# Delta-rule recurrence on one core: beta-k reads the state, the inverse is applied in compact form, and each step's data comes in one record

## The reference, cut to what matters

```python
T = jnp.tril(Bi @ KiT, k=-1)
inv = jnp.linalg.inv(eyeC + T)
Ui = inv @ (Vi - Bi @ W_t)
W_new = W_t + KiT @ Ui
...
O_i = Qi @ W_avg * a + Qi @ W_t * c + T_mat * (Qi @ KiT) @ Ui
```

## Time and profile before

| what | us |
|---|---|
| median of three runs | 1509.95 |
| lowest and highest of them | 1496.23, 1513.25 |
| the profiled execution, its own time | 1498.91 |
| its span, first to last instruction | 1497.1 |

### The profile page before, as it was taken

How to read it: one execution, slowest core, us unless ns; L and a number is a source line. 1 busy time by engine, 2 the same in 40 slices (tenths; PEclk the granted TensorE clock), 3 DMA queues, 4 the chain that set the end, 5 groups by cost and what they waited for, 6 DMA issues and landing times. The chain is left out here.

```text
span 1497.1 us, 35306 instructions
## 1 busy us (share of the span) xinstructions
PE 1164.3 (78%) x14558; PEld 796.8 (53%) x14558; DVE 749.3 (50%) x1707; ACT 452.9 (30%) x889; POOL 321.9 (22%) x309
## 2 busy tenths in 40 slices
PE   4843765665655067778887878999999999999997
PEld 2632434434444056666676764665566666666664
DVE  4689999899999436754444453112111121211111
ACT  3540534424435022222332323331122222222221
POOL 3686101000000011110011104661022222222222
PEclk9875777778778557687888878999999999999999
DMA  7642555464556676567665619952132222223222
GB/s 272 189 145 63 147 153 116 132 162 103 143 111 158 160 158 152 130 143 165 157 148 141 160 56 342 346 167 78 28 47 47 46 47 44 46 47 47 47 46 29
DMA packets 232444, 184.00 MB, mean 123 GB/s; under 512 B 148165, under 2 KB 196197, under 8 KB 227937
## 3 DMA queue, kind: packets, MB, share of 16 engines
q1 hardware_dynamic: 198000, 149.20, 38.0%
q0 software_dynamic: 16368, 19.96, 7.6%
q10 hardware_dynamic: 17920, 12.59, 3.1%
HBM read 101.69 MB, written 86.26 MB: 126 GB/s over the span
## 5 line engine op out<-in xcount | busy, mean ns | idle before, releaser
L1420 DVE TENSOR_TENSOR hid_all<-p_s,silu 128x512 f32<-128x512 f32 x103 | 71.3, 692 | 378.5 <-PE p_s L1271 249.7
L1470 POOL DMA_INDIRECT out_h<-y_sb,x_in x71 | 110.8, 1560 | 360.7 <-DVE y_sb L1432 342.8
L1328 ACT ACTIVATE silu<-p_m 128x512 f32<-128x512 f32 x103 | 61.5, 597 | 328.2 <-PE p_m L1264 223.4
L175 DVE TENSOR_TENSOR xt<-xt,prod 128x62 f32<-128x62 f32 (+15 forms) x248 | 151.8, 612 | 4.3
L1286 PE MATMUL p_y<-wo,hid_all 128*128 x568 | 134.4, 380 | 0.8 <-ACT hid_all L1345 0.8
L1264 PE MATMUL p_m<-wi,xT_c 128*128 x284 | 133.6, 593 | 0.5 <-ACT xT_c L1341 0.5
L1271 PE MATMUL p_s<-ws,xT_c 128*128 x284 | 133.6, 593 | 0.0
L172 DVE TENSOR_TENSOR prod<-nx,xt 128x62 f32<-128x62 f32 (+15 forms) x248 | 129.6, 523 | 2.6
L577 DVE SCALAR_TENSOR_TENSOR cv<-raw,conv_sb,cv 128x512 f32<-128x512 f32 x144 | 107.0, 747 | 18.0 <-ACT raw L493 17.2
L1286 PEld LDWEIGHTS p_y<-wo,hid_all 128*128 128x128 f32 x568 | 102.5, 190 | 12.3 <-issue 1.4
L452 PE MATMUL p_g<-kqM,kT 32*32 32x128 f32 x2048 | 50.7, 369 | 71.2 <-DVE sT L647 53.8
(11 more groups left out here) (139 smaller groups left out, 1938.0 us busy)
## 6 DMA issues: line engine op xcount, KB each, us to landing
slots_in_dram<-h SPq DMA_DIRECT2D x9, 1040.0 KB, 10.0
x_in<-slots_in_dram SPq DMA_DIRECT2D x71, 130.0 KB, 2.1
k_tokens_dram<-kk SPq DMA_DIRECT2D x32, 256.0 KB
chunk_gram_dram<-ng SPq DMA_DIRECT2D x32, 256.0 KB
beta_kv_dram<-bv SPq DMA_DIRECT2D x32, 256.0 KB
nx<-chunk_gram_dram SPq DMA_DIRECT2D x8, 1024.0 KB, 4.9
xt<-in_const SPq DMA_DIRECT2D x8, 1024.0 KB, 8.0
scores_dram<-sT SPq DMA_DIRECT2D x32, 256.0 KB
```

Source lines behind the costliest of these rows:

```text
L175: ins = dve.tensor_tensor(kept, kept, pr, ALU.add)
L1420: dve.tensor_tensor(dst, p_s[n % 2][:], silu[n % 2][:], ALU.mult).then_inc(S["hid_ready"], 1)
L1470: pool.indirect_dma_start(token_rows, bass.IndirectOffsetOnAxis(x_in[s % X_IN][:, D:D + 1].bitcast(U32), 0), y_sb[s % 2][:], None, compute ...
```

## The change

- The projections make beta k and beta v in tensors of their own (`bk`, `bv`). After `gram(b, 1)` TensorE transposes beta k (`turn_beta_k`, 8 transposes into `p_p`), ScalarE copies it out with a minus sign into `nkT` (two copies of 128x512), and SP stores it by channels (`kT_dram`, four stores of 128 KB) after the scores. `project(b + 1, 0)` and `project(b + 1, 1)` wait for these copies in place of those of `kk`.
- k with its copy, scores, inverse and beta v of a chunk lie beside each other in one DRAM tensor: a record of 1792 f32 (7168 B) for each token.
- A step's record comes in one transfer into one of three buffers (`load_record`), after `inside` of three steps earlier. Every fourth step `load_kq` issues 4 loads of minus beta k by channels and 8 of q. POOL now zeroes `nk`, and only the first `load_kq` waits for it.
- `read_k(s)` multiplies minus beta k by the state into `p_r`; VectorE adds beta v (`rho_out`); `apply(s)` multiplies the compact transposed inverse by the result, one 32x32 product for each head and lane, into `p_u`. In chunk 0 there is no `read_k`, and `apply` takes beta v itself.
- `yz`, `take_z`, `read_y`, `yz_out`, `xbd`, and the constants that pick z and sign y go. `turn_xn` uses `p_r`.
- The orders change: `read_k`, `read_q` before `route`; `turn_xn` ahead of `project`; `norm` a step later; `head_norm` ahead of `residual`; `store_inverse` of the last sequence at s = 12 in place of 14.

The diff, cut to its core:

```diff
+AT_KK, AT_SCORES, AT_INVERSE, AT_BV, RECORD = 0, 2 * D, 2 * D + H * C, 2 * D + 2 * H * C, 3 * D + 2 * H * C
...
+    step_dram = nc.dram_tensor("step_records_dram", [NC_BATCH, B, C, RECORD], F32, kind="Internal").ap()
...
                         sp.wait_ge(s_sT, b * TILES + TILES)
-                        by_chunk(sT_dram, b, sT[:].rearrange("p t g x -> p t (g x)"), s_st)
+                        by_chunk(AT_SCORES, b, sT[:].rearrange("p t g x -> p t (g x)"), H * C)
+                        sp.wait_ge(s_nk, b * 2 + 2)
+                        by_slot(kT_dram, b, nkT)
...
                         elif b:
-                            pe.wait_ge(s_kt, (b - 1) * 2 + n + 1)
-                            pe.wait_ge(s_ktri, (b - 1) * TILES + 2 * (n + 1))
+                            pe.wait_ge(s_nk, (b - 1) * 2 + n + 1)
...
+                    def turn_beta_k(b):
+                        for u in range(2):
+                            pe.wait_ge(s_kt, b * 2 + u + 1)
+                            pe.wait_ge(s_ktri, b * TILES + 2 * (u + 1))
+                            pe.wait_ge(s_bk, b * 2 + u + 1)
+                            for s in range(4):
+                                t, k = 2 * u + s // 2, s % 2
+                                ins = pe.transpose(p_p[u][:, s * P:(s + 1) * P], bk[:, t, k * P:(k + 1) * P], ident)
+                            ins.then_inc(s_bkt, 1)
...
                         gram(b, 1)
+                        turn_beta_k(b)
...
+                        for u in range(2):
+                            act.wait_ge(s_bkt, b * 2 + u + 1)
+                            act.activation(nkT[:, :, 2 * u * P:(2 * u + 2) * P].rearrange("p k (t l) -> p t k l", t=2),
+                                           p_p[u][:].rearrange("p (t k l) -> p t k l", t=2, k=KH), ACT.Copy, scale=-1.0
+                                           ).then_inc(s_nk, 1)
...
+                        for f in range(4):
+                            sp.dma_start(nk[i][C * f:C * f + DH], kT_dram[n // TILES, n % TILES, f * DH:(f + 1) * DH]).then_inc(s_nk[i], 16)
...
+                    def load_record(s):
+                        if s >= RING:
+                            sp.wait_ge(S["o_summed"], s - RING + 1)
+                        b = s // NC_BATCH * GROUP
+                        sp.dma_start(record[s % RING][:], step_dram[chunk(s), b:b + GROUP].rearrange("b i x -> (b i) x")
+                                     ).then_inc(s_rec[s % RING], 16)
...
-                        load_yz(s)
-                        load_kk(s)
-                        load_scores(s)
+                        load_record(s)
                         if s == 0:
-                            load_q(0)
+                            sp.wait_ge(s_zeroed, 2)
+                            load_kq(0)
...
+                    def read_k(s):
+                        if chunk(s) == 0:
+                            return
+                        n4 = s // TILES
+                        pe.wait_ge(s_nk[n4 % 2], 16 * 4 * (n4 // 2 + 1))
+                        pe.wait_ge(S["state_ready"], 2 * states(s - 1))
+                        if s >= 3:
+                            pe.wait_ge(S["xnT_ready"], s - 2)
+                        tok = slice(s % TILES * C, s % TILES * C + C)
                         for n in range(HQ):
-                            for f in range(4):
-                                ins = pe.matmul(p_yz[C * f:C * f + C, n, :], bv[s % 2][:, 4 * n + f, :], xbd[s % 2][:, 4 * n + f, :],
-                                                start=True, stop=True)
-                        ins.then_inc(S["yz_summed"], 1)
+                            for b in range(GROUP):
+                                ins = pe.matmul(p_rf[lane(b), n * 4 * DH:(n + 1) * 4 * DH], nk[n4 % 2][:, b, n, tok],
+                                                state[s % 2][:, b, n, :], start=(n == 0), stop=True, skip_group_check=True)
+                        ins.then_inc(S["r_summed"], 1)
...
+                    def apply(s):
+                        pe.wait_ge(s_rec[s % RING], 16 * (s // RING + 1))
+                        if chunk(s):
+                            pe.wait_ge(S["rho_ready"], reads(s))
                         if s:
                             pe.wait_ge(S["u_ready"], s)
-                        for n in range(HQ):
+                        src = rho[s % 2] if chunk(s) else bv[s % RING]
+                        for hd in range(H):
                             for b in range(GROUP):
-                                ins = pe.matmul(p_u[lane(b), n * 4 * DH:(n + 1) * 4 * DH], yz_ch[s % 2][:, n, lane(b)], table("pick_z"),
-                                                start=(n == 0), stop=False, skip_group_check=True)
...
+                                ins = pe.matmul(p_u[lane(b), hd * DH:(hd + 1) * DH], xT[s % RING][lane(b), hd, :],
+                                                src[lane(b), hd * DH:(hd + 1) * DH], start=(hd == 0), stop=True, skip_group_check=True)
                         ins.then_inc(S["u_summed"], 1)
...
-                    yz(0)
-                    take_z(0)
                     for s in range(NT + 4):
+                        if s < NT:
+                            read_k(s)
+                            read_q(s)
                         if s >= 4:
                             route(s - 4)
                         if s < NT:
-                            read_y(s)
-                            read_q(s)
+                            apply(s)
                         if 1 <= s <= NT:
                             turn_o(s - 1)
                         if s < NT:
                             grow(s)
-                            if s + 1 < NT:
-                                yz(s + 1)
                             inside(s)
+                        if 2 <= s < NT + 2:
+                            turn_xn(s - 2)
                         if 1 <= s <= NT:
                             project(s - 1)
-                        if s + 1 < NT:
-                            take_z(s + 1)
-                        if 2 <= s < NT + 2:
-                            turn_xn(s - 2)
...
+                    def rho_out(s):
+                        if chunk(s) == 0:
+                            return
+                        dve.wait_ge(S["r_summed"], reads(s))
+                        dve.wait_ge(s_rec[s % RING], 16 * (s // RING + 1))
+                        if s >= 2:
+                            dve.wait_ge(S["u_summed"], s - 1)
+                        dve.tensor_tensor(rho[s % 2][:], p_rf, bv[s % RING], ALU.add).then_inc(S["rho_ready"], 1)
...
                     for s in range(NT + 4):
+                        if s < NT:
+                            rho_out(s)
+                        solve(SHARE * s)
+                        if 2 <= s < NT + 2:
+                            norm(s - 2)
                         if s >= 4:
                             gate(s - 4)
-                        solve(SHARE * s)
+                        solve(SHARE * s + 2)
                         if s < NT:
                             state_out(s)
+                            solve(SHARE * s + 4)
                             head_sum(s)
-                        solve(SHARE * s + 2)
+                            solve(SHARE * s + 6)
+                            head_norm(s)
                         if 1 <= s <= NT:
                             residual(s - 1)
-                        solve(SHARE * s + 4)
-                        if s < NT:
-                            head_norm(s)
-                        solve(SHARE * s + 6)
-                        if 1 <= s <= NT:
-                            norm(s - 1)
```

196 lines of the change are left out of this document (75 added, 121 removed).

## The result

The changed kernel takes 1566.86 us (median of four runs, 1565.13 to 1570.09) against 1506.69 for the kernel before, measured beside it (four runs, 1496.23 to 1513.25): a ratio of 1.041, with an interval of 1.034 to 1.047. The prediction was 1522, with a range to 1560.

A forecast was written before the change was run, and what follows sets the result against it. TensorE waiting for blocks of 256 instructions was taken to bound the recurrence. +22 us there and net 0 at its start (projections' +4 included) on 1498.9 gave about 1520, 1531 on the median's footing; stated 1522, range 1484 to 1560.

The forecast's parts named there:

- the median's footing: Whole kernel: the sum counted from the three-run median 1509.95 us, not the profiled execution's 1498.9, giving 1531.
- point 1: Recurrence: TensorE groups removed 95.6 us, added 75.0, so busy time falls by 20.6 us, 0.66 us a step.
- point 2: Recurrence: 128 more TensorE instructions a step, 22,912 in place of 18,816, so 91 block refills for 74 or 75.
- point 3: Recurrence: the refill sets the pace almost always; 89 blocks at 4.05 us are 360 us, +22; bounds -13 and +71.
- The clock: Recurrence: more time at the lower clock lengthens work, not refills, which still set the pace; no change counted.
- point 5: Recurrence loads: one record transfer and three buffers gain 0 directly, add no wait; VectorE's new order costs nothing.
- fourth rival: Recurrence: 7 KB record rows hold refills up, 4.6 us a block, +71, 1570 us; chance 0.08.
- points 4 and 5: Recurrence: `read_q`'s 5.0 us wait for o_n goes, not counted as gain; VectorE's new order costed at nothing.
- points 6 and 7: Projections: beta k's transposes and added stores cost together +4 us; recurrence start: net 0, bounds -5 and +3.
- within 1%: Whole kernel: time within 1% of the median shown, from the even case and the forecast's low end; chance 0.33.
- the forecast: Recurrence: 3.98 to 4.3 us a block, 1514 to 1545 around 1522 us; chance 0.37.
- the even case: Recurrence: at 3.85 to 3.95 us a block work and instructions cancel, +4 to +13, about 1506; chance 0.28.

The follow-up runs named there:

- later runs: The kernels before and after, both unedited, profiled again beside the follow-up experiments: 1541.45 us (0.999) and 1598.86 us (1.036).
- b_plus128: Kernel before with 32 more groups of 32x32 products (128 instructions) behind `inside` in each step, results unread: 1602.34 us, ratio 1.040.
- a_minus128: Kernel after with `inside` for 8 of its 16 heads except in chunk 0, 128 instructions a step less: 1566.39 us, ratio 1.014.
- b_same: Kernel before, unedited, measured and profiled again beside the follow-up experiments: 1541.45 us, ratio 0.999.
- a_diag: Kernel after with `apply` as 16 products 128x128 by 128x16 with the block-diagonal inverse, in place of 64 small ones: 1649.38 us, ratio 1.069.
- b_narrow: Kernel before with `project` on 64 of its 256 columns, as many instructions: 1545.95 us, ratio 1.000.
- b_merged: Kernel before with VectorE's new order, without `take_z`; VectorE puts the pick of z into a second, negated state: 1552.58 us, ratio 1.005.
- a_apart: Kernel after with `read_q` behind `apply`, and `turn_xn` and `project` between `grow` and `inside`, same instructions: 1652.60 us, ratio 1.070.
- a_four: Kernel after with each record loaded in four transfers (pieces of 2, 2, 2 and 1 KB), same bytes: 1582.99 us, ratio 1.024.
- a_quiet: Kernel after without the record loads of steps 3 to 31, which reuse the records of steps 0 to 2: 1579.96 us, ratio 1.023.
- b_record: Kernel before, own algorithm, with one record of 8 KB rows in one transfer a step, three buffers, POOL spreading the inverse: 1552.56 us, ratio 1.005.
- b_order_fill: Kernel before with VectorE's new order and one unread product 128x128 by 128x256 more in each step: 1540.22 us, ratio 0.998.

## Why the prediction was wrong

The direction was as written; the size was short by 45 us (1567 for 1522), beyond the range to 1560. 1522 was itself a step between two footings: the sum on the median's footing was 1531, and on that footing 36 us are missing.

- *TensorE's work* (point 1): removed and added groups came out 20 us apart in the later runs, as worked out. That the busy sum of the stage would fall by 20 us was wrong: +47 in the first profiles, +25 in the later ones.
- *Instructions* (point 2): 89 packets for the 91 forecast, gaps in `apply` and `inside`, 90.7 us of issue for "80 or more". Right. (The "about 745" instructions a step do not follow from the count beside it: 22,912 over 32 steps are 716; the trace has 721.)
- *The price of a block* (point 3): the sum said +22 us. b_plus128 gives 16.7 us of waiting for 15 blocks, a_minus128 gives 9.6. The size was near, but not by the mechanism: "the refill sets the pace almost always" was wrong. Only 47 of the 89 blocks were waited for, and between them stand stretches such as the one of 5.85 us in which TensorE never stops. TensorE is busy 320.5 of the 407.3 us, so longer work lengthens the stage too; a step took 13.6 us, not 11.5 to 12. The page "Runtime: NRT & Kernel Launch" of the Trainium skill, in its section on instruction fetch mechanics, has the fetch hidden by the issue rate; the traces of this case disagree: b_same has 44.3 us of issue waits in 28 places, and even a_diag, which has the fewest, 16.4 us in 14.
- *The clock* is the step that failed: "A larger share at the lower level lengthens work, not refills, and the refill still sets the pace; I count no change". In its place the runs show that the lower clock (0.60 for 0.79 in the first profiles, 0.62 for 0.74 in the later ones) lengthened the groups that stay by 44 us in the later runs, and that the refills did not cover it: busy time rose by 24.8 us net, and the rest did not fall but rose by 34.9. The earlier trace rows gave 0.77 and the earlier trace rows windows from 1.00 down to 0.78, so both levels were in the trace of before, and `grow` at both of its durations too: the price of a full fall could have been bounded from it. What in the change makes the clock fall stays open. b_narrow and b_merged show a fall when work is narrowed or taken out in the kernel before, and this change does take work out; a_apart shows one with more waits and another order, and the change brings more waits as well. No run parts the two in the kernel after.
- *One transfer* (point 5): "Gain 0 directly" was wrong by a cost of 16 us. That cost rests on a_four and a_quiet; in b_record, with the algorithm of before, 8 KB rows cost next to nothing. The fourth rival, big packets, had +71 and 1570 us, and the profiles show +72.0 and the median 1567. That is luck: by the runs the transfer accounts for about 16 us of it, and the clock, which that rival does not have, for more. The second half, three buffers, was right: 0.
- *VectorE's order* (points 4 and 5): put at nothing, gave 6 to 9 us in the kernel before. The waits for o_n, said to go, are 3.4 us in three places in the profile of after, for 5.0.
- *Projections and start* (points 6 and 7): +4 and 0 were forecast. The channel loads' buffer is zeroed 6.3 us earlier than the old one (509.63 for 515.89 in the earlier trace rows), and the second u comes 2.2 us earlier (541.36 for 543.62), 6.9 in the later runs. But the first u comes 3.0 us later (531.26 for 528.28), near the +4 forecast, and 4.2 earlier in the later runs. A small miss to the good side, not clear of the difference between executions.
- *The chances*: "within 1%" of 1509.95 reaches to 1525, so it holds the forecast's own centre, 1522; giving it only the even case and 0.05 of the forecast doesn't follow. And the forecast's range is 1514 to 1545 in one place, 1508 to 1545 in another.

By parts, in the later runs: 20 us of work less, 44 for the lower clock, 10 to 17 for 15 more blocks, 16 for the transfer, 7 less from the start. That is +43 to +50 for a measured +57. The gain of VectorE's order showed itself as busy time at a higher clock, so it lies within the 44 if it is there at all. The parts were measured one at a time, most of them in one kernel only, and need not add.

## What to carry to other kernels

Before counting removed TensorE work as a gain, or as hidden, look at the granted clock of the stage and price the groups that stay at the lower level too: here that was the largest term. Count instructions and look for gaps at every 256th, but a block costs what its wait shows (1 us on average in the kernel after), not its full interval. In a loop that has many such waits, try several transfers in 1 to 2 KB pieces against one in 7 KB rows (16 us here), and take the parts of a large change singly: VectorE's order alone was 0.7% faster while the whole was 4% slower.

## What the runs showed that I had not expected

- TensorE busy 95% of 447 us at a mean granted clock of 0.59 (a_diag), and busy 83% at 0.84 (b_order_fill): of these two the busier stage had the lower clock.
- 24 us of short waits more (a_apart) went with 0.09 less of clock and 29 us more of work.
- 128 small instructions a step cost little more than half as much to wait for when taken away from the kernel after (9.6 us) as when added to the kernel before (16.7).
- The same kernel took 1506.69 us in the first measurement and about 1545 in all later ones. Up to the first u its clock was 0.73 for 0.76, in the thirty steps 0.74 for 0.79. The ratio of the change was 1.041 and 1.036.
